# Two attention stages: the multiplication by the reciprocals on VectorE, and eleven of sixteen blocks pooled on GpSimd

## The reference

```
x = x + tanh(g_xattn[0]) * L0_xattn(layernorm(x), ctx)   # causal self attention + attention over ctx, 16 heads of 32
x = x + tanh(g_ffn[0])   * L0_ffn(layernorm(x))          # 8 experts, each takes the top k tokens
x = x + tanh(g_xattn[1]) * L1_xattn(layernorm(x), ctx)   # attention over ctx, 16 heads of 32
x = x + tanh(g_ffn[1])   * L1_ffn(layernorm(x))          # 8 experts, twice the tokens
attention: softmax(q @ k.T * scale) @ v per head, then a projection
```

## Time and profile before

| | |
|---|---|
| median of 3 runs | 4030.9 us (4030.63 to 4036.47) |
| the profiled execution's own time | 4039.2 us |
| its span in the profile | 4037.5 us |
| busy TensorE / VectorE / ScalarE / GpSimd | 3698.3 / 2506.9 / 2060.4 / 1770.6 us |
| mean granted clock of TensorE | 0.953 of full speed |

### The profile page before, as it was taken

One profiled execution on the slowest core, in us unless ns is written; L12 is line 12 of the kernel. 1 busy time (PEld: TensorE's weight loads), 2 busy tenths in 40 slices (PEclk: granted clock), 3 DMA queues, 4 the chain that ended last, 5 costly groups with the idle time before them and its releaser, 6 DMA issues. The chain is left out here.

```text
span 4037.5 us, 76143 instructions
## 1 busy us (share of the span) xinstructions
PE 3698.3 (92%) x30244; PEld 2594.3 (64%) x30244; DVE 2506.9 (62%) x2873; ACT 2060.4 (51%) x3649; POOL 1770.6 (44%) x874
## 2 busy tenths in 40 slices
PE   6989699999999998869996699999998859999998
PEld 5768456666665664459995355555554548888886
DVE  4345687878888784666664677777773553333342
ACT  2222266666666665146662366666665144444432
POOL 0000287687778777002110488888886011111110
PEclk9999799999999999879998799999999869999999
DMA  4478724424442431636653522222211423333341
GB/s 160 166 235 296 203 77 104 109 74 105 98 114 59 110 87 45 227 118 201 219 186 115 148 78 79 75 80 78 76 44 55 174 87 117 117 117 108 115 113 38
DMA packets 290266, 485.13 MB, mean 120 GB/s; under 512 B 23104, under 2 KB 121408, under 8 KB 287936
## 3 DMA queue, kind: packets, MB, share of 16 engines
q1 hardware_dynamic: 274368, 443.01, 36.5%
q0 software_dynamic: 14080, 37.76, 4.1%
q10 hardware_dynamic: 1536, 0.40, 0.1%
HBM read 350.67 MB, written 130.02 MB: 119 GB/s over the span
## 5 line engine op out<-in xcount | busy, mean ns | idle before, releaser
L803 ACT ACTIVATE attn_probs<-attn_low 128x512 f32<-128x512 f32 (+1 forms) x2368 | 1234.6, 595 | 467.4 <-PE attn_low L714 351.7
L844 DVE TENSOR_REDUCE attn_parts<-attn_mx 128x4 f32<-128x2048 f32 x538 | 1232.8, 2291 | 366.3 <-PE attn_mx L686 365.6
L665 POOL TENSOR_TENSOR attn_psums<-attn_psums,attn_probs 128x1024 f32<-128x1024 f32 x536 | 1275.1, 2379 | 66.6 <-ACT attn_probs L803 1.4
L714 PE MATMUL attn_low<-attn_queries,attn_keys 97*128 97x256 f32 (+1 forms) x4736 | 914.7, 311 | 13.5 <-ACT attn_probs L803 5.5
L714 PEld LDWEIGHTS attn_low<-attn_queries,attn_keys 97*128 97x128 f32 x4736 | 658.3, 190 | 371.7 <-ACT attn_probs L803 187.7
L731 PE MATMUL attn_low<-attn_probs,attn_values 128*32 128x256 f32 x9472 | 629.4, 383 | 1.4 <-ACT attn_probs L803 1.4
L1528 DVE TENSOR_TENSOR ring_low<-ring_raw,ring_high 128x2048 fp32r<-128x2048 f32 x128 | 293.1, 2292 | 206.7 <-ACT ring_high L1485 206.7
L662 POOL TENSOR_TENSOR attn_psums<-attn_probs 128x1024 f32<-128x1024 f32 x88 | 209.6, 2382 | 371.6 <-ACT attn_probs L803 371.6
L731 PEld LDWEIGHTS attn_low<-attn_probs,attn_values 128*32 128x32 f32 x9472 | 247.6, 109 | 182.8 <-issue 2.1
L1442 PE MATMUL ffn_up<-ffn_xH,ring_high 128*128 128x256 f32 (+1 forms) x1024 | 351.0, 343 | 2.7 <-DVE ffn_xL L1534 2.7
L1442 PE MATMUL ffn_up<-ffn_xH,ring_low 128*128 128x256 f32 (+1 forms) x1024 | 348.2, 340 | 0.0
(11 more groups left out here) (200 smaller groups left out, 4434.6 us busy)
## 6 DMA issues: line engine op xcount, KB each, us to landing
ring_raw<-in_L_ffn_W_dram SPq DMA_DIRECT2D x128, 1024.0 KB, 5.5
attn_keys<-l_cross_keys SPq DMA_DIRECT2D x96, 512.0 KB, 6.9
attn_queries<-l_queries SPq DMA_DIRECT2D x48, 512.0 KB, 4.8
l_cross_keys<-projc_high SPq DMA_DIRECT2D x64, 256.0 KB, 2.2
l_cross_keys<-projc_lowp SPq DMA_DIRECT2D x64, 256.0 KB, 2.4
l_cross_values<-projc_vout SPq DMA_DIRECT2D x64, 256.0 KB, 2.5
attn_keysn<-l_cross_keys SPq DMA_DIRECT2D x16, 1024.0 KB, 5.0
attn_values<-l_cross_values SPq DMA_DIRECT2D x32, 512.0 KB, 8.3
```

The source lines that it names most:

```text
L665: pool.tensor_tensor(ps, ps, at, ALU.add).then_inc(added, 1)
L714: mm = pe.matmul(out[:, n0:], KS[b][0:3 * HD + 1, h, kb * P:(kb + 1) * P], QS[b][0:3 * HD + 1, h, job.qb * QB + n0:(job.qb + 1) * QB], sta ...
L803: act.activation(probs[:, m % RING, i // 2, heads, n0:], sc[:, item % SC, :].rearrange("p (h q) -> p h q", q=QB)[:, :, n0:], ACT.Exp, scal ...
L844: op = dve.tensor_reduce(into, seen, AX.X, ALU.max)
```

## The change

The block 9 joins the pooled ones of a context job: eleven pooled blocks, ten sums, and five blocks for L738. The causal jobs keep theirs. GpSimd's loop has no normalization any more. VectorE does it instead, in the same step `m = end + 6`, behind that step's maxima and behind the fourth piece of the reciprocals, which it computed a step earlier. The waits are the same: the four pieces, and the store of five jobs before.

```
         else:
-            self.pooled = [kb for kb in whole[:-3] if kb < 4 or kb == 7 or kb % 2 == 0]
+            self.pooled = [kb for kb in whole[:-3] if kb < 4 or kb in (7, 9) or kb % 2 == 0]
...
-                def normalize(j):
-                    d = j % DEEP
-                    pool.wait_ge(inverted[d], PIECES * (j // DEEP + 1))
-                    if j >= DEEP:
-                        pool.wait_ge(y_out[d], DMA * (j // DEEP))
-                    pool.tensor_tensor(y[d][:, :], both[d][:, 0, :], inv[d][:, :], ALU.mult).then_inc(normed, 1)
-
-                for m in range(N_STEPS + 8):
-                    if 0 <= m - 6 < N_STEPS and plan.ends(m - 6) is not None:
-                        normalize(plan.ends(m - 6))
-                    if m >= N_STEPS:
-                        continue
+                for m in range(N_STEPS):
                     j = plan.job_of[m]
...
+                def normalize(j):
+                    d = j % DEEP
+                    dve.wait_ge(inverted[d], PIECES * (j // DEEP + 1))
+                    if j >= DEEP:
+                        dve.wait_ge(y_out[d], DMA * (j // DEEP))
+                    dve.tensor_tensor(y[d][:, :], both[d][:, 0, :], inv[d][:, :], ALU.mult).then_inc(normed, 1)
...
-                for m in range(N_STEPS + 6):
+                for m in range(N_STEPS + 7):
                     if m < N_STEPS:
                         for k in plan.groups_at[m]:
                             reduce(k)
                     for piece in range(PIECES):
                         if 0 <= m - 2 - piece < N_STEPS and plan.ends(m - 2 - piece) is not None:
                             invert(plan.ends(m - 2 - piece), piece)
+                    if 0 <= m - 6 < N_STEPS and plan.ends(m - 6) is not None:
+                        normalize(plan.ends(m - 6))
```

## The result

The changed kernel took 4156.6 us (median of 4 runs, 4148.7 to 4162.8) against 4031.6 for the kernel before (4030.6 to 4036.5) beside it: a ratio of 1.0301 [1.0288, 1.0314], slower by 125 us. The forecast was 86 us more, with a range that ended at 4140. The sign and the chain of ten sums were right; the size was not. The profiled execution took 4161.0 (span 4159.0), 121.8 over the one before.

The account below looks back on a forecast made before the run. TensorE was taken to bound the kernel before, GpSimd's chain of ten sums after. The chain's +66 and contention's +20 made +86, on the median of 4030.9 a forecast of 4117 us, range 4086 to 4140.

Parts of the forecast that it names:

- The bound and the chain: Context jobs: GpSimd's ten sums become the bound, 25.1 from first sum to closing matmul, against TensorE's 23.93.
- the ring: Three probability buffers: step 7 waits for block 9's sum, which alone puts the closing matmul at some 24.8.
- a few tenths at least: Sign: L746 idle for GpSimd by this much in nearly every context job.
- The tenth sum: One more GpSimd sum per context job: 68.4 over jobs, less 2 in causal jobs, +66 before contention.
- a gain of 2: Causal jobs: ScalarE's exponents wait less for GpSimd's sums, counted as -2 (0 to -8).
- Fourth jobs: Stage 0's fourth context jobs, seven of them: 0.35 us more each, taken between 0.25 and 0.6, 2.5 in all.
- Contention of the two engines: Context jobs: a VectorE product slips between GpSimd sums and delays the next by 0.28; 71 times, 20 us.
- hidden with 0.5 to spare: VectorE in a context job's step 5: the product's 0.42 fits while VectorE waits for TensorE's next maxima.
- the rival's first case: VectorE loses the lock: product waits one sum, harmless; losing again costs 0.5 per job, 35, 4150. Chance 0.09.
- the 71 meetings: Products meeting a context job's chain: 5 per unit in stage 0 (two in the first job), 31 in stage 1.
- the whole possible gain: TensorE: removing block 9's ones matmuls saves 0.55 us per context job, 64 times, 35 us.
- asks no earlier than before: The store on SP, with the product on VectorE, is requested no earlier; no cost counted.

Follow-up runs that it names:

- both_step6_hold: Changed kernel (eleven pooled blocks) with context jobs' products in step 6 and SyncE's store and loads held: 4122.2 against 4035.1 for the kernel before, 1.0219.
- move_step6_hold: Ten pooled blocks, product on VectorE in step 6 for context jobs, SyncE's store and loads held: 4039.5 us, 1.0006 of the kernel before.
- move_only: Product on VectorE as in the changed kernel, but ten pooled blocks as before: 4097.4 against 4036.3 for the kernel before, 1.0148.
- late_product: Changed kernel with third and fourth causal jobs' products moved to steps 5 and 6 of the first context job, stores one step later: 4119.1 us, 1.0208.
- opened: Eleven pooled blocks, products in step 6, next job's block 3 scores and exponent moved ahead at a job's end: 4093.7 us, 1.0153 of the kernel before.
- before_opened: Kernel before with only the order at a job's end changed, as in opened: 4100.1 us, 1.0169 of the kernel before.
- move_hold: move_only with SyncE holding a context job's store and later loads until the next job's step 6 values products: 4071.3 against 4038.7, 1.0086.
- move_step6: Ten pooled blocks, product on VectorE in step 6 for context jobs, last two causal jobs' in steps 5 and 6: 4058.3 against 4032.4, 1.0068.

## Why the prediction was off

**The bound and the chain** were right: 25.1 from first sum to closing matmul was forecast, and 25.10 to 25.15 came in 24 of 32 jobs of stage 1, with a period of 27.0. TensorE doesn't gain from less work, because the ring and the chain hold it: it waits 0.6 for step 7's exponents and then 0.1 for the last sum, and not "a few tenths at least" for the last sum as the signs said.

**The tenth sum was +66 by the forecast and is about +87** (both_step6_hold, with the moved product at no cost by move_step6_hold). The table finds 84 of the 87. Its excess over the forecast is 8 in the middle of stage 1, where six jobs ran partly at the lower clock behind a wait that the chain itself makes; 6 in the causal jobs, where a gain of 2 had been counted and 4 were lost (2.6 of them in one job, in which TensorE waits 1.34 and the clock falls; why was not taken apart); and 6 in the context jobs of stage 0, less 2.5 in stage 1's first. Fourth jobs came as forecast (25.2 in the changed kernel, at 25.22). The prediction counted the wait and not what the clock does behind it.

**The step that failed is "Contention of the two engines"**, the term 71 x 0.28 = 20, with the sentence before it that the product is "hidden with 0.5 to spare". The runs showed some 38 in its place (125 - 87), and nearly all of it in eight jobs. Three things were wrong in it:
- *Who waits.* Nine sums in a row last 22.54 with a product beside them, so GpSimd paid 0 there and not 0.28. VectorE pays, up to a whole sum (2.39), in 78 of 96 products. The row that I rested on the earlier trace rows was of an indirect DMA, and a sum doesn't behave like it. The Trainium skill ("SBUF — State Buffer", section "SBUF: two separate sides") says that the first to start keeps the ports for its whole instruction. With sums 0.14 apart that is nearly always GpSimd, and the 2.36 at 819.30 agrees. The case that the forecast took for the usual one occurs once in the changed kernel: a product begins in the gap, 0.09 before a sum, and the sum takes 2.56 (VectorE, then GpSimd):

```profile
1137.73 0.41 DVE L858 TENSOR_TENSOR attn_y<-attn_both,attn_inv 128x256 f32<-128x256 f32 x1
```

```profile
1137.82 2.56 POOL L654 TENSOR_TENSOR attn_psums<-attn_psums,attn_probs 128x1024 f32<-128x1024 f32 x1
```

- *Where it decides.* I took step 5 of a context job for all products. In stage 1 the wait is harmless there (0.98, maxima at once behind it): the rival's first case, and its price of 0.5 a job didn't arise. (That rival's time was also added up wrong: 4031 + 66 + 35 is 4132, not 4150, so that 4150 lies nearer to the 4157 measured is luck.) Products of third causal jobs fall into the second step of the first context job, where VectorE had 0.16 of idle time in a step. I had counted that product among the 71 meetings, and never looked at VectorE's row there. In five of these eight jobs the next product, in step 5, then meets a sum from its start too.
- *What it costs.* It is not the 2.09 of waiting alone but the clock behind it and the second wait: 28.3 to 34.2 per job, where a job with the wait and a full clock took 25.95 (move_only). late_product takes this away and gives 37.5 back in these jobs.

So +125 is about 87 for the tenth sum and 38 for products, nearly all in the first context jobs, in place of 66 and 20. The 5 us of the clock that rises late at the start of stage 0 are in the profiled execution of the changed kernel, and a few us of such differences are in each of these numbers. That the forecast of 86 for both parts is the +87 of the tenth sum alone is chance.

**Block 9's ones matmuls, "the whole possible gain" of 35**, were oversized as well. A step without ones matmuls is bound by the loop of the maxima, not by TensorE's own work, and opened against before_opened gives 0.3 a job: 20 us at most. It did not enter the sum, because the chain took it all.

**The store** "asks no earlier than before" was wrong too: in the rows of SyncE above it is issued 15.3 behind a job's first sum (2541.37) in move_only, and 18.2 behind it (2593.10) in the kernel before. With ten blocks that alone costs some 28 us (move_only against move_hold). With eleven it doesn't show: stage 1 lost 39.1 with the early store and 40.6 with the held one, probably since TensorE waits for the chain there anyway.

## What to carry to other kernels

A small instruction moved to an engine that has to wait for its neighbour can cost what the neighbour's instruction lasts, not its own length. Look up for every place where it lands, and not for the typical one, what its new engine has to spare and who waits behind it. Where one of the two engines never pauses for more than a gap between its instructions, it is nearly always the other one that waits, and the trace writes the wait into the duration, not into idle time. A wait of a microsecond or two on TensorE is to be priced with the clock that may follow it. An instruction that releases a queue of loads moves these loads too.

## What the runs showed of the hardware

- A product of 128x256 on VectorE lasts 0.36 alone and up to 2.39 beside sums on GpSimd (2.59 in opened, as the second of two in a row); with one input 0.23 and up to 2.38. In the changed kernel one that begins inside a sum ends 0.28 to 0.36 behind that sum.
- GpSimd's sums kept 2.34 to 2.40 in all but 8 of 688 cases in the changed kernel. Those eight, of 2.44 to 2.56, start while a product is at work: seven begin 0.20 to 0.23 after a product that was asking already, and the one of 2.56 begins 0.09 after a product that began in the gap. In move_step6_hold, where more products come just before a sum, 43 sums are longer than 2.40, up to 2.59.
- After TensorE's idle 2.1 in a first context job the granted clock came back at the 1.2 GHz level in all eight jobs of the changed kernel, and stayed there for a time that differs: one job of 28.3 had a mean of 0.94, one of 34.1 a mean of 0.70. In move_only two of eight jobs with the same wait stayed at 1.00. After a wait of 0.6 it fell in four to seven jobs of stage 1, at distances of four jobs or a multiple of four, and not in the others.
- The same first job of stage 0 ran at the 2.4 GHz level from 485 us in the kernel before and from about 496 in the changed one, which made 5.0 us. TensorE had been busy alike up to then (10.36 and 10.37 us of 460 to 480, 4.82 of 480 to 485).
- The DMAs of two small rows landed up to 1.36 us late for TensorE in move_only, where SyncE had issued a store and a load of keys shortly before them, and up to 2.06 late in move_step6, where the store and a load were issued 0.13 and 0.57 behind the first of them (589.68). In the kernel before they are issued 0.57 and 0.96 behind it (2610.75), and TensorE has no such wait there. With the store and the loads held back, one wait of more than 0.5 us is left in move_hold.
